# Bucket sums of layer two of a four-layer graph network: blocks of four tiles, added in PSUM by TensorE

## The chip, the cores and the metric

The kernel runs on one core of a Trainium2 chip. The metric is the device time of one execution, in microseconds (us). Before the change it is 17409.68 us, the median of three runs (17409.63 to 17410.06).

## The reference, cut to what matters

Four message-passing layers run on one graph of 12,500 nodes and 400,000 edges sorted by destination. Each layer reads node rows by an index, makes a message per edge, sums the messages per target node, adds the result to `x` and normalises. Layers one, three and four sum by `dst`, which is sorted. Layer two (`_L1_gnn_ref`) is different: it reads by `dst` and sums by `src`, which is random.

```python
edge_index = jnp.stack([src, dst])
# layer two
xj = x[edge_index[1]]
msg = basis[:, 0:1] * (xj @ w2[0])
for k in range(1, k1 * k2):
    msg = msg + basis[:, k:k + 1] * (xj @ w2[k])
out = jax.ops.segment_sum(msg, edge_index[0], num_segments=n_nodes)
```

## The kernel before, in words

Layer two takes two passes. The first (the spread) computes the 32 numbers of each message and scatters the row (33 numbers: the message and the target's number inside its bucket) to a table `pay` in HBM. The nodes are split into 125 buckets of 100; a bucket has some 3,200 edges. Each bucket owns whole tiles of 128 rows there. Rows that no edge fills hold the number -1 and add nothing. These filler rows are written during layer one by SyncE's queue (L2138). The spread is a loop of 125 chunks; its scatters are issued by GpSimd, 25 for each chunk (L1898).

The second pass (the fold) is what the change is about. The tiles are read back in four groups side by side, 825 tiles to a group (`Q1`), in 33 chunks of 25 tiles (`T`) per group. For each tile a one-hot matrix of 128 rows by 100 nodes is made, and TensorE multiplies the 32 message columns with it, which gives 32x100 sums; the four groups are the four column groups of the array, so one tile of each group fills 128 partitions of PSUM (L1728). VectorE then carries a running sum along the tiles: `row[t] = row[t-1] * ms[t] + product[t]`, where `ms` is 0 at the start of a bucket (`vector_sums2`, L783). Each chunk's rows go to a table `fold` in HBM (L1394), from which GpSimd later gathers the last row of each bucket (L1994).

A chunk is worked in five blocks of five tiles (times four groups, 20 one-hots of 100 columns). VectorE makes a block's one-hots in one instruction (L770, 128x2000). ScalarE needs 20 small instructions (L1384) and one large one (L1387). GpSimd needs 20 small ones (L1920). In chunks with an odd number VectorE makes blocks 0, 2, 4, GpSimd block 1 and ScalarE block 3; in even ones VectorE makes 0 and 4, GpSimd 1, ScalarE 2 and 3. There are two row buffers, one one-hot buffer for each block, and four PSUM banks, taken in turn.

The order is written out by hand: each engine has its own program, which waits on counters. `q_y` counts blocks that TensorE has finished, `dv` counts VectorE's instructions (`PER2` of them in a chunk), `q_a` ScalarE's blocks and `po_rows` GpSimd's. TensorE goes through the blocks in order; before a block it waits for its one-hots and for VectorE to have read the bank. A row buffer is loaded again (SyncE's queue, L2092) when TensorE is done with the chunk two before. The buckets' tile numbers are computed on VectorE in `vector_starts` between layers one and two (L596 to L634).

Of the kernel before, what the change touches and what calls it, by code (L numbers as in the profile page):

```python
# [27 lines left out]
Q1 = 825  # L28
NT1 = 4 * Q1
NC1 = Q1 // T  # L30
# [36 lines left out]
def gnn_kernel(nc, x, src, dst, ea2, ea3, ea5, ew, ew1, W0, W1, G2, MU, SG, ROOT, BIAS, w1, b1, w2, b2, out):  # L67

    ctx = ExitStack()
    with ctx:  # L70
# [22 lines left out]
        til_d = dram("til", [NP * 27])  # L93
        fold_d = dram("fold", [P * Q1, NJ])
# [130 lines left out]
        kc = cv(Q1)  # L225
        hb_ = cv(625)
        tot, tls, cum, bst = cv(125), cv(125), cv(125), cv(125)
        tid_i, tid = cv(27, I32), cv(27)
        tilb = cv(27)
        gof, lst = cv(4), cv(2)  # L230
        tli = cv(125, I32)
        big = cv(27 * 25)[0:NP]
# [35 lines left out]
        F1.rows = [cv(4 * 33 * T) for _ in range(2)]  # L268
        F1.rowv = [a.rearrange("p (g t c) -> p g t c", g=4, c=33) for a in F1.rows]
        F1.OH = [cv(20 * NJ) for _ in range(2)]  # L270
        F1.row = [cv(T * NJ) for _ in range(2)]
        F1.ms = [cv(T) for _ in range(2)]
        F1.tail = cv(NJ * 32)[0:3]
        F1.crossT = cv(NP)[0:3]
        F1.OH += [cv(20 * NJ) for _ in range(3)]
        F1.OHv = [a.rearrange("p (g t n) -> p g t n", g=4, t=5) for a in F1.OH]
# [161 lines left out]
        def vector_between(e):  # L438
# [127 lines left out]
        def vector_starts(e):  # L566
# [5 lines left out]
            e.tensor_scalar(tot, tot, 127.0, None, ALU.add).then_inc(dv.up(), 1)  # L572
# [3 lines left out]
            e.tensor_scalar(tli, tli, 7, None, ALU.arith_shift_right).then_inc(dv.up(), 1)  # L576
# [8 lines left out]
            e.tensor_scalar(bst, bst, 128.0, None, ALU.mult).then_inc(dv.up(), 1)  # L585
# [10 lines left out]
            for b in range(0, 125, 25):  # L596
                after(e)
                e.tensor_tensor(
                    big.rearrange("p (t b) -> p t b", t=27), cum[0:NP, b:b + 25].unsqueeze(1).to_broadcast([NP, 27, 25]),
                    tid[0:NP].unsqueeze(2).to_broadcast([NP, 27, 25]), ALU.is_le).then_inc(dv.up(), 1)  # L600
                after(e)
                e.tensor_reduce(bst[0:NP, 0:27], big.rearrange("p (t b) -> p t b", t=27), AX.X, ALU.add).then_inc(dv.up(), 1)
                after(e)
                if b == 0:
                    e.tensor_copy(tilb[0:NP], bst[0:NP, 0:27]).then_inc(dv.up(), 1)
                else:
                    e.tensor_tensor(tilb[0:NP], tilb[0:NP], bst[0:NP, 0:27], ALU.add).then_inc(dv.up(), 1)
# [8 lines left out]
            for r in range(3):  # L616
                e.tensor_scalar(gof[0:NP, r:r + 1], lst[0:NP, 0:1], float(Q1 * (r + 1)), None, ALU.is_ge).then_inc(dv.up(), 1)
                e.tensor_scalar(cross[0:NP, r:r + 1], gof[0:NP, 3:4], float(Q1 * (r + 1) - 1), None, ALU.is_le).then_inc(dv.up(), 1)
# [4 lines left out]
            e.scalar_tensor_tensor(out=lst[0:NP, 0:1], in0=mean[0:NP, 0:1], scalar=float(31 * Q1), in1=lst[0:NP, 0:1], op0=ALU.mult, op1=ALU.add).then_inc(dv.up(), 1)  # L623
# [5 lines left out]
            e.tensor_scalar(var[0:NP, 0:32], io125[0:NP, 0:32], float(Q1), lst[0:NP, 0:1], ALU.mult, ALU.add).then_inc(dv.up(), 1)  # L629
# [3 lines left out]
            e.tensor_tensor(xr[:, 1:Q1], kc[:, 1:Q1], kc[:, 0:Q1 - 1], ALU.is_equal).then_inc(dv.up(), 1)  # L633
# [120 lines left out]
        PER2 = 28  # L754

        def v2_rows(c, b):
            return c * PER2 + (mk["base2"] + {0: 1, 2: 7, 4: 13}[b])

        def v2_sum(c, b):
            return c * PER2 + (mk["base2"] + {0: 12, 1: 18, 2: 23, 3: 28, 4: 34}[b])  # L760

        def numbers2(k, b):

            return F1.rowv[k % 2][:, :, 5 * b:5 * b + 5, 32:33]

        def vector_rows2(e, c, i, k, b):
            if b == 0:
                e.wait_ge(sem(f"ro1_{k % 2}"), nth2(i, k) * 16)
            e.wait_ge(sem("q_y"), c * 5 + (b + 6))
            e.tensor_tensor(F1.OHv[b], numbers2(k, b).to_broadcast([P, 4, 5, NJ]),  # L770
                            iop[:, 0:NJ].unsqueeze(1).unsqueeze(1).to_broadcast([P, 4, 5, NJ]), ALU.is_equal).then_inc(dv.up(), 1)

        def vector_sums2(e, c, i, k, b):
            s2 = k % 2
            e.wait_ge(sem("q_y"), c * 5 + (b + 11))
            if b == 0:
                e.wait_ge(sem("q_m"), c + 1)
                e.wait_ge(sem(f"rowd1_{s2}"), nth2(i, k) * 16)
            for j in range(5):
                t = 5 * b + j  # L780
                so_far = F1.row[s2][:, NJ * t - NJ:NJ * t] if t else F1.row[1 - s2][:, NJ * T - NJ:NJ * T]
                e.wait_ge(dv.h, v2_sum(c, b) - (5 - j) if j else (v2_sum(c, b - 1) if b else v2_sum(c - 1, 4)))
                e.scalar_tensor_tensor(out=F1.row[s2][:, NJ * t:NJ * t + NJ], in0=so_far, scalar=F1.ms[s2][:, t:t + 1],  # L783
                                       in1=ps[(k + b) % 4][:, NJ * j:NJ * j + NJ], op0=ALU.mult, op1=ALU.add).then_inc(dv.up(), 1)

        def vector_chunk2(e, c, i, k):
            i_ = 0 if i is None else i
            vector_rows2(e, c, i_, k, 0)
            if i is None:
                e.wait_ge(dv.h, v2_rows(0, 0))  # L790
                e.sem_inc(dv.up(5), 5)
            else:
                vector_sums2(e, c - 1, i, k - 1, 4)

            vector_rows2(e, c, i_, k, 2 if k % 2 else 4)
            vector_sums2(e, c, i_, k, 0)
            if k % 2:
                vector_rows2(e, c, i_, k, 4)
            else:
                e.wait_ge(dv.h, v2_rows(c, 4) - 1)  # L800
                e.sem_inc(dv.up(), 1)
            for b in range(1, 4):
                vector_sums2(e, c, i_, k, b)

        def vector_fold(e):
# [4 lines left out]
            vector_chunk2(e, 0, None, 0)  # L810
            with e.Fori(0, NC1 // 4) as i:
                for k in range(1, 5):
                    vector_chunk2(e, i * 4 + k, i, k)
            e.wait_ge(dv.h, v2_sum(NC1 - 1, 3))
            e.sem_inc(dv.h, 1)
            vector_sums2(e, NC1 - 1, NC1 // 4 - 1, 4, 4)
            dv.n = v2_sum(NC1 - 1, 4)

# [555 lines left out]
        def scalar_chunk2(e, c, i, k):  # L1374
            s2 = k % 2
            e.wait_ge(dv.h, v2_sum(c - 2, 4))
            e.activation(F1.ms[s2], xr[:, bass.ds(c * T, T)], ACT.Copy).then_inc(sem("q_m"), 1)

            e.wait_ge(sem(f"ro1_{s2}"), nth2(0 if i is None else i, k) * 16)
            for b in (3,) if k % 2 else (2, 3):  # L1380
                e.wait_ge(sem("q_y"), c * 5 + (b + 6))
                for g in range(4):
                    for j in range(5):
                        m = e.activation(F1.OHv[b][:, g, j], io125[:, 0:NJ], ACT.Abs, scale=-1.0, bias=F1.rowv[s2][:, g, 5 * b + j, 32:33])  # L1384
                m.then_inc(sem("q_d"), 1 + k % 2)
                e.wait_ge(sem("q_d"), c * 2 + (b - 1))
                e.activation(F1.OH[b], F1.OH[b], ACT.Relu, scale=-1.0, bias=ones[:, 0:1]).then_inc(sem("q_a"), 1 + k % 2)  # L1387
# [328 lines left out]
        def tensor_chunk2(e, c, k):  # L1716
            s2 = k % 2
            for b in range(5):
                if b in (0, 4) or b == 2 and k % 2:
                    e.wait_ge(dv.h, v2_rows(c, b if k % 2 or b == 0 else 2))  # L1720
                elif b == 1:
                    e.wait_ge(sem("po_rows"), c + 2)
                else:
                    e.wait_ge(sem("q_a"), c * 2 + (b - 1))
                e.wait_ge(dv.h, v2_sum(c, 0) if b == 4 else v2_sum(c - 1, b + 1))
                for j in range(5):
                    for g in range(4):
                        m = e.matmul(ps[(k + b) % 4][32 * g:32 * g + 32, NJ * j:NJ * j + NJ], F1.rowv[s2][:, g, 5 * b + j, 0:32],  # L1728
                                     F1.OHv[b][:, g, j], start=True, stop=True)
                m.then_inc(sem("q_y"), 1)  # L1730

        def tensor_fold(e):
            e.sem_inc(sem("q_y"), 10)
# [177 lines left out]
        def gpsimd_chunk2(e, c, i, k):  # L1911

            s2 = k % 2
            e.wait_ge(sem(f"ro1_{s2}"), nth2(0 if i is None else i, k) * 16)
            held(e)
            e.wait_ge(sem("q_y"), c * 5 + 7)
            held(e)
            for g in range(4):
                for j in range(5):
                    m = e.tensor_scalar(F1.OHv[1][:, g, j], io125[:, 0:NJ], F1.rowv[s2][:, g, 5 + j, 32:33], None, ALU.is_equal)  # L1920
# [344 lines left out]
```

## Time and profile before

| | us |
|---|---|
| median of the runs shown | 17409.68 |
| the profiled execution's own time | 17404.72 |
| its span, first to last instruction | 17402.7 |
| layer one and its ends | up to 4411 |
| the spread | 4411 to 8435 |
| the fold, first load issued to last sum | 8440.2 to 8921.2 |
| layers three and four | from 8975 |

Over the span, VectorE is busy 70%, GpSimd 74%, TensorE 37% and ScalarE 19%. These shares are means over stages that have different limits: in the spread GpSimd issues scatters without a pause, in layer four VectorE and TensorE are busy. Only the fold's own rows speak of the fold.

### The profile page before, as it was taken

The numbers are of one execution on the slowest core, as the hardware profiler recorded it, in microseconds if no ns is written. First come the engines' busy times: TensorE is split into PE (matmuls) and PEld (weight loads), VectorE is DVE, ScalarE is ACT, GpSimd is POOL, SyncE is SP. The second block draws the span as 40 slices with busy tenths as digits, with TensorE's granted clock in tenths as the row PEclk, the third lists the DMA queues.
The fourth block names the chain that finished last, engine by engine and source line by source line (L and its number), as shares of the span: only waits on it lengthen the run. The fifth ranks groups of instructions, "written<-read, shape, count | busy, mean of one in ns | idle before, by whom it ended". The sixth has DMA issues, their size and how long they took to land. (4 is left out here: it accounts for less than half of the span.)

```text
span 17402.7 us, 138752 instructions
## 1 busy us (share of the span) xinstructions
PE 6419.3 (37%) x33487; PEld 5142.6 (30%) x33487; DVE 12117.7 (70%) x15588; ACT 3285.1 (19%) x5336; POOL 12932.6 (74%) x13715
## 2 busy tenths in 40 slices
PE   1000000000444454545330000000006999999995
PEld 0000000000333333333320000000005878878774
DVE  5666666674899999999663232223326999999996
ACT  0000000000222222222541101111102223222321
POOL 6777777777677777777757777777777777777776
PEclk9555555555777777777665555555558999999998
DMA  4333333331111111111332222222222222222221
GB/s 103 97 96 97 97 98 97 98 97 47 28 28 28 28 28 28 28 28 25 130 130 59 59 57 59 58 59 58 59 53 45 55 55 53 56 53 56 53 56 36
DMA packets 744244, 1076.69 MB, mean 62 GB/s; under 512 B 375703, under 2 KB 508493, under 8 KB 731294
## 3 DMA queue, kind: packets, MB, share of 16 engines
q0 software_dynamic: 417376, 477.82, 12.5%
q1 hardware_dynamic: 250851, 398.14, 8.2%
q10 hardware_dynamic: 75736, 197.70, 3.1%
q8 instruction: 88, 1.44, 0.0%
q14 instruction: 193, 1.58, 0.0%
HBM read 684.92 MB, written 389.48 MB: 62 GB/s over the span
## 5 line engine op out<-in xcount | busy, mean ns | idle before, releaser
L1937 POOL DMA_INDIRECT s_arena<-d_t,s_arena x3125 | 3086.5, 988 | 971.3 <-issue 943.6
L1898 POOL DMA_INDIRECT d_pay<-s_arena x3125 | 3026.9, 969 | 997.7 <-issue 931.0
L1977 POOL DMA_INDIRECT s_arena<-d_t,s_arena x3125 | 2960.6, 947 | 1032.6 <-issue 952.0
L1955 POOL DMA_INDIRECT s_arena<-d_t,s_arena x3125 | 2948.5, 944 | 981.7 <-issue 952.1
L1649 PE MATMUL psall<-s_arena 128*128 128x500 bf16 x1875 | 835.4, 500 | 4365.4 <-DVE psall L881 3637.1
L992 DVE TENSOR_TENSOR s_arena<-s_arena,psall 128x2400 f32<-128x2400 f32 x125 | 332.0, 2656 | 2712.1 <-DMA s_arena<-d_t,s_arena 2712.1
L1649 PEld LDWEIGHTS psall<-s_arena 128*128 128x128 bf16 x1875 | 222.5, 119 | 4783.3 <-DVE psall L881 3708.7
L1756 PE MATMUL psall<-s_w2r,s_arena 128*128 128x384 f32 x4250 | 1514.0, 491 | 5.9 <-DVE s_arena L1090 5.2
L1838 PE MATMUL psall<-s_tails,s_mfix 128*128 128x32 f32 x6 | 1.9, 412 | 3972.8 <-DVE s_tails L1198 3972.8
L1756 PEld LDWEIGHTS psall<-s_w2r,s_arena 128*128 128x128 f32 x4250 | 1271.0, 317 | 64.3 <-DVE s_arena L1090 6.1
L1099 DVE TENSOR_REDUCE s_arena<-s_arena 128x64 f32<-128x1024 f32 x875 | 1248.1, 1438 | 0.0
L1838 PEld LDWEIGHTS psall<-s_tails,s_mfix 128*128 128x128 f32 x6 | 1.5, 313 | 3974.0 <-DVE s_tails L1198 3974.0
L1666 PE MATMUL psall<-s_ident,s_arena 128*128 128x128 f32 x3125 | 603.3, 321 | 1406.8 <-DVE s_arena L665 1406.8
L1675 PE MATMUL psall<-s_arena 128*128 128x128 f32 x6250 | 1052.1, 316 | 112.3 <-ACT s_arena L1360 103.5
L901 DVE TENSOR_REDUCE s_arena<-s_arena 128x600 f32<-128x4200 f32 x125 | 1027.2, 8218 | 4.3
L1360 ACT ACTIVATE s_arena<-psall 128x512 f32<-128x512 f32 x875 | 482.7, 552 | 2743.3 <-PE psall L1666 2743.3
L1675 PEld LDWEIGHTS psall<-s_arena 128*128 128x128 f32 x6250 | 906.0, 221 | 309.7 <-DVE s_arena L688 150.6
L564 DVE TENSOR_TENSOR s_arena<-s_arena,psall 128x625 bf16<-128x625 f32 x1250 | 957.7, 801 | 0.0
L890 DVE TENSOR_TENSOR s_arena<-s_arena,psall 128x600 f32<-128x600 f32 x125 | 97.5, 780 | 1172.4 <-DMA s_arena<-d_t,s_arena 1172.4
L1783 PE MATMUL psall<-s_arena,s_ident 128*128 128x256 f32 x4000 | 907.4, 378 | 0.0
L1666 PEld LDWEIGHTS psall<-s_ident,s_arena 128*128 128x128 f32 x3125 | 451.9, 168 | 1430.0 <-issue 1430.0
L1512 ACT ACTIVATE s_arena<-s_arena 128x800 f32<-128x800 f32 x125 | 213.9, 1711 | 3492.9 <-DVE psall L864 3463.7
(304 smaller groups left out, 17923.9 us busy)
## 6 DMA issues: line engine op xcount, KB each, us to landing
s_arena<-d_t,s_arena POOLq DMA_INDIRECT x9375, 2.5
d_scan<-s_arena ACTq DMA_DIRECT2D x313, 400.0 KB, 2.6
s_arena<-d_ew SPq DMA_DIRECT2D x126, 800.0 KB
s_arena<-d_pay SPq DMA_DIRECT2D x33, 1650.0 KB, 6.8
d_inj<-s_agg SPq DMA_DIRECT2D x125, 400.0 KB, 3.9
s_arena<-d_inj SPq DMA_DIRECT2D x125, 400.0 KB, 3.4
d_pay<-s_arena POOLq DMA_INDIRECT x3125, 2.2
d_fold<-s_arena ACTq DMA_DIRECT2D x33, 1250.0 KB, 4.9
```

The source lines that it names most:

```text
L564: return e.tensor_tensor(O[sl], h5[:, :, bass.ds(n, 1)].to_broadcast([P, 5, 125]), iob, ALU.is_equal)
L901: e.tensor_reduce(S[:, :, 8:32], w7.rearrange("p m t c -> p t c m"), AX.X, ALU.add)
L1099: e.tensor_reduce(L3.sums[s2][:, t0:t0 + n].rearrange("p t c -> p (t c)"), prod(g).rearrange("p t (b v) -> p (t b) v", v=16), AX.X, ALU.ad ...
L1649: e.matmul(R5s[:, 0:4], lhsT, rhs[:, 0:4], start=start, stop=True, skip_group_check=True)
L1666: m = e.transpose(ps[6][:, 128 * t:128 * t + 128], S1.xb[:, 128 * (t0 + t):128 * (t0 + t) + 128], ident[:, :])
L1675: m = e.matmul(ps[2 + yb][:, 128 * t:128 * t + 128], S1.xT[yb][:, 128 * t:128 * t + 128], S1.wt, start=True, stop=True)
L1756: m = e.matmul(ps[BANK[g] + t][:, 0:384], hv_[:, :, t0 + t], L3.w2v if g in ONPE else w2r[:, :], start=True, stop=True)
L1783: m = e.matmul(L3.vs, ident[:, :], L3.prodP[:, v], start=v == 0, stop=v == 15, skip_group_check=True)
L1898: e.indirect_dma_start(pay_d, bass.IndirectOffsetOnAxis(ap=S1.adr[s4][:, t:t + 1], axis=0), S1.pay[s4][:, 33 * t:33 * t + 33], None).then_ ...
L1937: e.indirect_dma_start(L3.gb[s][:, t], None, T3_d, bass.IndirectOffsetOnAxis(ap=L3.idx[s][:, t:t + 1], axis=0)).then_inc(sem(f"g3_{s}"), 16)
L1955: e.indirect_dma_start(L0.gb[s][:, t * 128:(t + 1) * 128], None, T0_d, bass.IndirectOffsetOnAxis(ap=L0.idx[s][:, t:t + 1], axis=0)).then_i ...
L1977: e.indirect_dma_start(L2.gb[k][:, t * 96:(t + 1) * 96], None, T2_d, bass.IndirectOffsetOnAxis(ap=L2.idx[k][:, t:t + 1], axis=0)).then_inc ...
```

## The change

A bucket now owns whole blocks of four tiles (512 rows; before it was whole tiles of 128). A chunk has seven blocks (`NBK`) of four tiles (`K4`) per group, 28 tiles; there are still 33 chunks (`NC1`), so the table grows from 3,300 to 3,696 tiles. TensorE adds the four products of a block in one place of PSUM (`start=j == 0`, `stop=j == K4 - 1`), and VectorE's running sum takes one instruction of 128x100 for a block, seven for a chunk. `fold` has seven entries per chunk and group, where it had 25.

The one-hots of a block are now 16 per instruction group (128x1600). In even chunks VectorE makes blocks 0 to 3, ScalarE 4 and 5, GpSimd 6; in odd ones VectorE 0 to 4, ScalarE 5, GpSimd 6. There are four row buffers, and eight one-hot buffers, of which the eighth is block 4's in even chunks. VectorE's sums of blocks 4, 5 and 6 of a chunk stand between its first one-hots of the next one. The fillers in layer one are 30 tiles a chunk, where they were 27. In `vector_starts` five passes of three instructions over 25 buckets become one of two over all 125.

```diff
-Q1 = 825
+K4 = 4
+NBK = 7
+NC1 = 33
+QBK = NBK * NC1
+Q1 = K4 * QBK
...
-        F1.rows = [cv(4 * 33 * T) for _ in range(2)]
+        F1.rows = [cv(4 * 33 * K4 * NBK) for _ in range(4)]
...
-            for b in range(0, 125, 25):
...
+            e.tensor_tensor(
+                big.rearrange("p (t b) -> p t b", t=NTI), cum[0:NP].unsqueeze(1).to_broadcast([NP, NTI, 125]),
+                tid[0:NP].unsqueeze(2).to_broadcast([NP, NTI, 125]), ALU.is_le).then_inc(dv.up(), 1)
...
+        PER2 = 12
+        BY_VECTOR = ((0, 1, 2, 3), (0, 1, 2, 3, 4))
+        BY_SCALAR = ((4, 5), (5,))
...
+        def bank2(k, b):
+
+            return ps[(3 * k + b) % 4]
 
         def vector_rows2(e, c, i, k, b):
             if b == 0:
-                e.wait_ge(sem(f"ro1_{k % 2}"), nth2(i, k) * 16)
-            e.wait_ge(sem("q_y"), c * 5 + (b + 6))
...
+                e.wait_ge(sem(f"ro1_{k % 4}"), nth4(i, k) * 16)
+            e.wait_ge(sem("q_y"), y2(c - 2, 4) if b == 4 else y2(c - 1, b))
+            e.tensor_tensor(F1.OHv[b], number2(k, b).to_broadcast([P, 4, K4, NJ]),
+                            iop[:, 0:NJ].unsqueeze(1).unsqueeze(1).to_broadcast([P, 4, K4, NJ]), ALU.is_equal).then_inc(dv.up(), 1)
+
+        def vector_sum2(e, c, i, k, b):
             s2 = k % 2
-            e.wait_ge(sem("q_y"), c * 5 + (b + 11))
+            e.wait_ge(sem("q_y"), y2(c, b))
...
-            for j in range(5):
...
+            e.wait_ge(dv.h, v2_sum(c, b - 1) if b else v2_sum(c - 1, NBK - 1))
+            e.scalar_tensor_tensor(out=F1.row[s2][:, NJ * b:NJ * b + NJ], in0=so_far, scalar=F1.ms[s2][:, b:b + 1],
+                                   in1=bank2(k, b)[:, 0:NJ], op0=ALU.mult, op1=ALU.add).then_inc(dv.up(), 1)
 
         def vector_chunk2(e, c, i, k):
             i_ = 0 if i is None else i
...
+            for b in range(3):
+                vector_rows2(e, c, i_, k, b)
+                if i is None:
+                    e.wait_ge(dv.h, v2_rows(c, b))
+                    e.sem_inc(dv.up(), 1)
+                else:
+                    vector_sum2(e, c - 1, i, k - 1, 4 + b)
+            vector_rows2(e, c, i_, k, 3)
+            vector_sum2(e, c, i_, k, 0)
+            if 4 in BY_VECTOR[k % 2]:
                 vector_rows2(e, c, i_, k, 4)
...
             for b in range(1, 4):
-                vector_sums2(e, c, i_, k, b)
+                vector_sum2(e, c, i_, k, b)
...
         def scalar_chunk2(e, c, i, k):
...
-            for b in (3,) if k % 2 else (2, 3):
...
+            for b in BY_SCALAR[k % 2]:
+                o = onehot2(k, b)
+                e.wait_ge(sem("q_y"), y2(c - 2, 4) if b == 4 else y2(c - 1, b))
...
         def tensor_chunk2(e, c, k):
...
+                e.wait_ge(dv.h, v2_sum(c, b - 4) if b > 3 else v2_sum(c - 1, b + 3))
+                for j in range(K4):
                     for g in range(4):
...
+                        m = e.matmul(bank2(k, b)[32 * g:32 * g + 32, 0:NJ], F1.rowv[k % 4][:, g, K4 * b + j, 0:32],
+                                     F1.OHv[o][:, g, j], start=j == 0, stop=j == K4 - 1, skip_group_check=True)
...
         def gpsimd_chunk2(e, c, i, k):
...
+            b = NBK - 1
...
+            e.wait_ge(sem("q_y"), y2(c - 1, b))
...
         def sync_chunk2(e, c, k):
...
-            e.wait_ge(sem("q_y"), c * 5 + 5)
...
+            e.wait_ge(sem("q_y"), y2(c - 4, NBK - 1))
```

On VectorE, at the start of a chunk inside the fold's loop, this stood before. `m_ro1_0` is the row load's counter, `m_q_y` TensorE's, `m_dv` VectorE's own.

```order
L768 ISA
L769 ISA [waits m_ro1_0]
L770 TENSOR_TENSOR s_arena<-s_arena,psall 128x2000 [waits m_q_y]
L775 REGISTER_ALU
L782 REGISTER_ALU [waits m_q_y]
L783 SCALAR_TENSOR_TENSOR s_arena<-s_arena,psall 128x100 [waits m_dv]
L782 REGISTER_ALU
L783 SCALAR_TENSOR_TENSOR s_arena<-s_arena,psall 128x100 [waits m_dv]
```

Five sums of the chunk before followed one block of one-hots. At the same place there is now one sum between two blocks:

```order
L781 TENSOR_TENSOR s_arena<-s_arena,psall 128x1600 [waits m_q_y,m_ro1_3]
L786 REGISTER_ALU
L791 REGISTER_ALU [waits m_q_y]
L792 SCALAR_TENSOR_TENSOR s_arena<-s_arena,psall 128x100 [waits m_dv]
L781 TENSOR_TENSOR s_arena<-s_arena,psall 128x1600 [waits m_q_y]
L786 REGISTER_ALU
```

So a single sum stands between large instructions, for blocks 4, 5 and 6 of the chunk before. Each sum has its own wait for TensorE, where one wait served five sums.

On TensorE, the first chunk of the fold read so before (`m_po_rows` is GpSimd's block, `m_q_a` ScalarE's):

```order
L1728 MATMUL psall<-s_arena 32x100 [waits m_bar,m_dv]
L1728 MATMUL psall<-s_arena 32x100 x19
L1728 MATMUL psall<-s_arena 32x100 [waits m_dv,m_po_rows]
L1728 MATMUL psall<-s_arena 32x100 x19
L1728 MATMUL psall<-s_arena 32x100 [waits m_dv,m_q_a]
```

And now, from the chunk's fourth block on:

```order
L1741 MATMUL psall<-s_arena 32x100 [waits m_dv]
L1741 MATMUL psall<-s_arena 32x100 x15
L1741 MATMUL psall<-s_arena 32x100 [waits m_dv,m_q_a]
L1741 MATMUL psall<-s_arena 32x100 x15
L1741 MATMUL psall<-s_arena 32x100 [waits m_dv,m_q_a]
L1741 MATMUL psall<-s_arena 32x100 x15
L1741 MATMUL psall<-s_arena 32x100 [waits m_dv,m_po_rows]
```

GpSimd's block moved from second to last, ScalarE's stand right ahead of it, and VectorE's come first.

## Rows read from the trace of the kernel before

**Rows 1.** The fold: us; PE, PEld, DVE, ACT, POOL busy; clock, DMA share, GB/s
```profile
8440.20:8921.20 481.00, 230.22 (x6600) 209.81 (x6600) 433.04 (x907) 376.07 (x1083) 335.50 (x660) 0.73 0.54 204
```
**Rows 2.** Groups of instructions by line in the fold, 8440 to 8925
```profile
L1920 POOL TENSOR_SCALAR s_arena<-s_io,s_arena 128x100 f32<-128x100 f32 x660 | 335.5, 531 | 144.8 <-PE psall L1728 124.3 <-DMA s_arena<-d_pay 20.5
L1384 ACT ACTIVATE s_arena<-s_io,s_arena 128x100 f32<-128x100 f32 x1000 | 274.0, 364 | 79.0 <-PE psall L1728 72.1 <-DMA s_arena<-d_pay 6.8
L783 DVE SCALAR_TENSOR_TENSOR s_arena<-s_arena,psall 128x100 f32<-128x100 f32 x825 | 262.6, 318 | 38.6 <-PE psall L1728 7.3 <-DVEq L801 4.9 <-DVE s_arena L783 0.5
L1728 PE MATMUL psall<-s_arena 128*32 128x100 f32 x6600 | 230.2, 314 | 354.3 <-DVE s_arena L770 194.9 <-DVEq L791 118.5 <-issue 15.7
L770 DVE TENSOR_TENSOR s_arena<-s_arena,psall 128x2000 f32<-128x2000 f32 x82 | 182.9, 2231 | 9.6 <-DMA s_arena<-d_pay 7.2 <-issue 2.2
L1387 ACT ACTIVATE s_arena<-s_arena,s_ones 128x2000 f32<-128x2000 f32 x50 | 98.2, 1963 | 2.7
L1377 ACT ACTIVATE s_arena<-s_xr 128x25 f32 x32 | 6.9, 216 | 15.6 <-DVE s_arena L783 14.4 <-issue 1.2
```
**Rows 3.** Instructions in order of time, two chunks of the fold, from 8593.6
```profile
8593.61 2.23 DVE L770 TENSOR_TENSOR s_arena<-s_arena,psall 128x2000 f32<-128x2000 f32 x1
...
8595.76 1.73 DVE L783 SCALAR_TENSOR_TENSOR s_arena<-s_arena,psall 128x100 f32<-128x100 f32 x5
...
8595.97 5.19 PE L1728 MATMUL psall<-s_arena 128*32 128x100 f32 x120 [5.03 <-DVE s_arena L770]
8597.40 2.23 DVE L770 TENSOR_TENSOR s_arena<-s_arena,psall 128x2000 f32<-128x2000 f32 x1
...
8599.76 10.17 POOL L1920 TENSOR_SCALAR s_arena<-s_io,s_arena 128x100 f32<-128x100 f32 x20 [3.58 <-PE psall L1728]
8600.41 1.96 ACT L1387 ACTIVATE s_arena<-s_arena,s_ones 128x2000 f32<-128x2000 f32 x1
...
8601.58 5.28 DVE L783 SCALAR_TENSOR_TENSOR s_arena<-s_arena,psall 128x100 f32<-128x100 f32 x15 [0.30 <-DVEq L801]
...
8602.50 1.95 PE L1728 MATMUL psall<-s_arena 128*32 128x100 f32 x80 [1.33 <-ACT s_arena L1387]
8603.64 5.49 ACT L1384 ACTIVATE s_arena<-s_io,s_arena 128x100 f32<-128x100 f32 x20 [1.16 <-PE psall L1728]
...
8616.51 5.27 DVE L783 SCALAR_TENSOR_TENSOR s_arena<-s_arena,psall 128x100 f32<-128x100 f32 x15
...
8616.72 1.08 PE L1728 MATMUL psall<-s_arena 128*32 128x100 f32 x40 [1.04 <-DVE s_arena L770]
...
8621.70 2.23 DVE L770 TENSOR_TENSOR s_arena<-s_arena,psall 128x2000 f32<-128x2000 f32 x1
```
**Rows 4.** Two stretches of 3.5 us of the fold, columns as in rows 1
```profile
8597.10:8600.60 3.50, 3.50 (x92) 3.50 (x88) 3.36 (x6) 3.47 (x14) 0.84 (x2) 0.50 0.08 29
...
8614.70:8618.20 3.50, 2.05 (x84) 1.61 (x76) 3.36 (x6) 3.32 (x13) 3.50 (x8) 1.00 0.03 10
```
**Rows 5.** The page's costliest groups: a smaller VectorE instruction of the same kind
```profile
L890 DVE TENSOR_TENSOR s_arena<-s_arena,psall 128x600 f32<-128x600 f32 x125 | 97.5, 780 | 1172.4 <-DMA s_arena<-d_t,s_arena 1172.4
```
**Rows 6.** Instructions in order of time, the start of the fold
```profile
8435.23 2.14 DVE L807 MEMSET s_arena<- 128x2500 f32 x1 [101.69 <-PEq L159]
8437.84 2.14 DVE L807 MEMSET s_arena<- 128x2500 f32 x1 [0.47 <-issue]
```
**Rows 7.** Time to landing of the fold's row loads (L2092)
```profile
DMA to landing us min/median/max: 6.7/6.8/10.1
```
**Rows 8.** DMA issues by line in the fold and in layer one: KB, us to landing
```profile
d_fold<-s_arena ACTq DMA_DIRECT2D x33, 1250.0 KB, 4.9
...
d_scan<-s_arena ACTq DMA_DIRECT2D x33, 400.0 KB, 2.8
```
**Rows 9.** VectorE's first instruction after `vector_starts`, in order of time
```profile
4165.33 1.03 DVE L1249 TENSOR_TENSOR s_x<-s_x,s_agg 125x768 f32<-125x768 f32 x1 [10.22 <-DMA s_agg<-d_scan,s_endi]
```
**Rows 10.** Who GpSimd waited for, 187 to 4440: total us, times, longest
```profile
POOL s_arena L1955 <- issue: 952.1, 3124, 0.3
```

More of the change, by code:

```diff
@@ L92, in gnn_kernel @@
         pay_d = dram("pay", [P * NT1, 33])
-        til_d = dram("til", [NP * 27])
-        fold_d = dram("fold", [P * Q1, NJ])
+        til_d = dram("til", [NP * NTI])
+        fold_d = dram("fold", [P * QBK, NJ])
         Y_d = dram("y", [P, (TP + T) * 9])
@@ L267, in gnn_kernel @@
         F1 = Spread()
[L268 removed]
+        F1.rows = [cv(4 * 33 * K4 * NBK) for _ in range(4)]
         F1.rowv = [a.rearrange("p (g t c) -> p g t c", g=4, c=33) for a in F1.rows]
[L270 to L272 removed]
+        F1.OH = [cv(4 * K4 * NJ) for _ in range(NBK + 1)]
+        F1.row = [cv(NBK * NJ) for _ in range(2)]
+        F1.ms = [cv(NBK) for _ in range(2)]
         F1.tail = cv(NJ * 32)[0:3]
         F1.crossT = cv(NP)[0:3]
[L275 to L276 removed]
+        F1.OHv = [a.rearrange("p (g t n) -> p g t n", g=4, t=K4) for a in F1.OH]
         assert cv.at <= ARENA
@@ L571, in vector_starts @@
             after(e)
-            e.tensor_scalar(tot, tot, 127.0, None, ALU.add).then_inc(dv.up(), 1)
+            e.tensor_scalar(tot, tot, float(128 * K4 - 1), None, ALU.add).then_inc(dv.up(), 1)
             after(e)
@@ L622, in vector_starts @@
             after(e)
-            e.scalar_tensor_tensor(out=lst[0:NP, 0:1], in0=mean[0:NP, 0:1], scalar=float(31 * Q1), in1=lst[0:NP, 0:1], op0=ALU.mult, op1=ALU.add).then_inc(dv.up(), 1)
+            e.scalar_tensor_tensor(out=lst[0:NP, 0:1], in0=mean[0:NP, 0:1], scalar=float(31 * QBK), in1=lst[0:NP, 0:1], op0=ALU.mult, op1=ALU.add).then_inc(dv.up(), 1)
             after(e)
@@ L813, in vector_fold @@
                     vector_chunk2(e, i * 4 + k, i, k)
[L814 to L817, printed above, removed]
+            for b in range(4, NBK):
+                e.wait_ge(dv.h, v2_sum(NC1 - 1, b - 1))
+                e.sem_inc(dv.h, 1)
+                vector_sum2(e, NC1 - 1, NC1 // 4 - 1, 4, b)
+            dv.n = v2_sum(NC1 - 1, NBK - 1)
         def vector_root(e, b):
@@ L1716, in tensor_chunk2 @@
         def tensor_chunk2(e, c, k):
[L1717 to L1721, printed above, removed]
+            for b in range(NBK):
+                o = onehot2(k, b)
+                if b in BY_VECTOR[k % 2]:
+                    e.wait_ge(dv.h, v2_rows(c, b))
+                elif b in BY_SCALAR[k % 2]:
+                    e.wait_ge(sem("q_a"), c * 2 + (b - 3))
+                else:
                     e.wait_ge(sem("po_rows"), c + 2)
[L1723 to L1726, printed above, removed]
+                e.wait_ge(dv.h, v2_sum(c, b - 4) if b > 3 else v2_sum(c - 1, b + 3))
+                for j in range(K4):
                     for g in range(4):
-                        m = e.matmul(ps[(k + b) % 4][32 * g:32 * g + 32, NJ * j:NJ * j + NJ], F1.rowv[s2][:, g, 5 * b + j, 0:32],
-                                     F1.OHv[b][:, g, j], start=True, stop=True)
+                        m = e.matmul(bank2(k, b)[32 * g:32 * g + 32, 0:NJ], F1.rowv[k % 4][:, g, K4 * b + j, 0:32],
+                                     F1.OHv[o][:, g, j], start=j == 0, stop=j == K4 - 1, skip_group_check=True)
                 m.then_inc(sem("q_y"), 1)
         def tensor_fold(e):
-            e.sem_inc(sem("q_y"), 10)
+            e.sem_inc(sem("q_y"), 3 * NBK)
             barrier(e, "tensor")
```

124 lines of the change are left out of this document (51 added, 73 removed).

## The prediction

> **What bounds the kernel now.** I first read the page's busy slices to find the stage, then the busy time of each engine inside it, then its groups of instructions, and last two chunks in order of time. The fold takes 481.0 us from the first load's issue to the last sum [rows 1]. In it VectorE is busy 433.0 us, which is 90%; ScalarE 78%, GpSimd 70%, TensorE 48%; the DMA engines have a share of 0.54. VectorE's own idle time is small: 38.6 us ahead of the sums and 9.6 ahead of the one-hots, against 354 us for TensorE and 145 for GpSimd, which wait for others [rows 2]. So VectorE sets the pace. Its time is 825 sums of 318 ns (262.6 us) and 82 blocks of one-hots of 2231 ns (182.9 us).
>
> In order of time the reader is to see the spacings, since starts overlap ends a little [rows 3]. A block of one-hots is followed after 2.15 us (8593.61 to 8595.76), 0.08 less than it lasts. Five sums in a row take 1.64 us until the next one-hots start (8595.76 to 8597.40), and fifteen take 5.19 (8616.51 to 8621.70). So one sum that feeds the next costs 0.351 us, and the last before a block of one-hots 0.24 (1.64 less four times 0.351). Two chunks are 28.09 us (8593.61 to 8621.70): five blocks of 2.15, 45 sums of 0.351 and five of 0.24 make 27.7, and one gap of 0.30 behind L801 the rest. This working leaves less than 0.1 us over, so I apply it to the new order.
>
> **VectorE after the change.** It makes nine blocks in two chunks, each 128x1600. No row has that size. Between 600 elements (780 ns) [rows 5] and 2000 (2231 ns) [rows 2] the slope is 1.036 ns, which gives 1816 ns; strict proportion to 2000 gives 1785, and the size left unchanged 2231. I take 1.815, so a spacing of 1.735: nine are 15.6 us. There are 14 sums. Seven stand alone ahead of one-hots (blocks 4, 5, 6 twice, block 0 in odd chunks): 7 x 0.24 = 1.7. The others are a run of four in even chunks and of three in odd ones: 5 x 0.351 + 2 x 0.24 = 2.2. The gap for a bare counter step (it was L801) stays in even chunks: 0.3. That is 19.8 us in two chunks, 9.9 in one, against 14.04.
>
> One new wait comes with it. In an even chunk the sum of block 3 stands right behind the one-hots of block 3, the sums of blocks 0 to 2 and the gap, some 1.3 us later. TensorE needs in that time 0.12 us to start (8595.84 to 8595.97), a block, and 0.1 to report. Forty instructions took 1.08 us with the clock at full (8616.72) [rows 3]; at 2.05 us for 84 [rows 4] eight fewer are 0.2 less, so a block of 32 is 0.9: 1.1 in all and no wait. At the lower level 92 took 3.50 us, 38 ns each [rows 4], so the block is 1.4, and VectorE waits 0.3. Queued behind that sum are the next chunk's one-hots, for which TensorE waits.
>
> The rows show both levels. A burst after 5.03 us of idle [rows 3] ran at 0.50, which is 1.2 GHz, and the one at 8616 at 1.00, which is 2.4 GHz [rows 4]; over the fold the mean is 0.73 [rows 1]. In the new order a block comes every 2 us or less and the long gaps go. The Trainium skill, "TensorE: Matmul & The Clock Gate", section "Loop structure matters more than you think", says that the loop nest decides whether matmuls stay warm, dense ones doing so and those split by waits running cold. By the rule as I read it dense blocks would hold the upper level and a chunk would take 9.9; if the bursts run as the one after idle did, 10.2.
>
> The mean clock lies between, and so do I: 10.05 us a chunk.
>
> **The other engines' loops, which must stay below that.** ScalarE makes three blocks in two chunks. Twenty small ones take 5.49 us [rows 3], 16 then 4.4; the large one 1.6 (from 216 ns at 25 elements and 1963 at 2000) [rows 2]: 6.0 a block, 18.0 for three. With two copies and one wait until TensorE frees the buffer of block 5 (relu's end at 8602.37 to 8603.64, 1.27 us for 40, so 1.1 for 32) [rows 3] it is 19.5 us in two chunks, under 20.1 by only 3%. GpSimd has one buffer: 16 of 20 in 10.17 us is 8.1, plus 0.2 to TensorE, its block and 0.2 back: 9.4 at full clock, 9.9 at the lower level. TensorE runs 7 x 32 = 224 instructions at 24 ns, 5.5 us (8.5 at 38). All are close behind VectorE, which is why my value isn't the 9.9.
>
> **Loads and stores.** A load is 28 tiles in place of 25, 1848 KB in place of 1650; landing goes from 6.8 [rows 7] to 7.6 us, bounded by 6.8 and, at its slowest of 10.1, by 11.3. With four buffers it has some 30 us, so it is hidden. A store shrinks from 1250 to 350 KB. The nearest row for one of that size is 400 KB in 2.8 us, against 4.9 for 1250 [rows 8]. Together the two move 2.2 MB where they moved 2.9, so the DMA engines get less to do in a chunk.
>
> **Start and end.** The first one-hots wait for the first load, 7.6 us. In chunk 0 ScalarE makes two blocks in a row, ready for VectorE at 7.6 + 12.0 + 1.1 = 20.7 us, where VectorE has got to 19.3: 1.4 us. The three sums at the end add 0.5. So the fold takes 33 x 10.05 + 9.5 = 341.2 us, against 481.0: 139.8 less. Ahead of it the barrier waits for two memsets of 2.14 us [rows 6], now of 700 elements: 0.6 each by size, 3.1 less. The last store lands some 2 us sooner [rows 8].
>
> **What costs nothing.** `vector_starts` loses 13 instructions, but VectorE stands idle for 10.22 us behind it, until a gather lands [rows 9]. The longer fillers, 30 tiles for 27, run beside GpSimd's gathers, which wait for nothing but their own issue in 3124 of 3125 cases [rows 10]; if that cover went, 50 KB more at 2.8 us for 400 KB [rows 8] would cost at most 0.35 us each, 44 us for 125. The spread's scatters are as many as before. The gathers from `fold` too.
>
> **Sum.** 139.8 + 3.1 + 2.0 = 144.9 less. The profiled execution took 17404.72 us in all, 17402.7 of it the span, and so gives 17259.8; the median of the runs shown is 5.0 above it. I predict 17265 us.
>
> **Rivals.** (a) ScalarE or GpSimd becomes the bound, each waiting in turn for TensorE, which takes blocks strictly in order. For it: ScalarE's 19.5 of 20.1. Against: their waits now (79.0 and 124.3 us) [rows 2] are time that they can give. At 10.8 us a chunk, with 0.75 x 33 = 25 us more, 17290. (b) The loads set the pace, four of them in flight beside the stores. At 11.3 us a chunk: 17306. Against it stands a share of 0.54 now. (c) Slower: adding in PSUM takes away the overlap of the four column groups, since an instruction that adds to a place must wait for the one before. An instruction would then take four times the 24.4 ns of 84 in 2.05 us [rows 4], 98 ns, and a chunk 224 x 98 ns = 21.9 us: 33 x 11.8 = 391 us over my forecast, 17656. It decides from 63 ns on, where 224 make 14.04 us. Against it: 3300 products are 6600 instructions now [rows 2], so each product is already made of two that add to one place. (d) It doesn't do what it says: the additions saved on VectorE come back as waits, so that a chunk stays at 13 or more. The gain is then under 35 us, 17375 or above. For it speaks only that every engine has one buffer per block; against, that no loop worked out above is over 10.2.
>
> **Chances.** My forecast, 9.7 to 10.4 us a chunk, 0.67; faster than that (shorter one-hots, the clock held) 0.07; (a) 0.15; (b) 0.04; (c) 0.04; (d) 0.03. A difference of 0.2% (35 us) is about what a measurement of this kernel can tell from no change. Faster is then 0.93, within it 0.03, slower 0.04. The range: 9.5 us a chunk gives 17247, and (a) up to 11.0 gives 17296; I take 17246 to 17300, which leaves out (c), (d), most of (b) and the ends of the others.
>
> **What would show it.** Right: VectorE over 92% busy in a fold of about 341 us, one-hots of 1.8 us, 231 sums, nine to two chunks in a steady pattern of one-hots, sum, one-hots; GpSimd and ScalarE waiting shortly for TensorE; the mean clock above 0.73. Wrong: VectorE's sums of blocks 5 or 6 waiting for TensorE, which would be (a); waits for the row loads, (b); a block of 32 on TensorE over 2 us, (c); a change in layers one, three or four.

## The result, and the profile after

The changed kernel takes 17329.07 us, the median of four runs (17328.70 to 17329.95), beside 17409.72 for the kernel before. The ratio is 0.9953 (0.9941 to 0.9965). It is faster by 80.6 us, where I forecast 144.9, and its time lies above my range. The profiled execution spans 17327.5 us, 75.2 less than before.

The fold, with the columns of [rows 1]:

```profile
8438.10:8844.50 406.40, 237.45 (x7392) 205.85 (x7392) 319.18 (x379) 302.64 (x883) 268.62 (x528) 0.78 0.52 185
```

It went from 481.0 to 406.4 us, and the forecast was 341.2. VectorE's 319 us of work fit the forecast (92% of 341 is 314), but they are 79% of the fold, where over 92% was expected. The groups by line answer to [rows 2]:

```profile
L1933 POOL TENSOR_SCALAR s_arena<-s_io,s_arena 128x100 f32<-128x100 f32 x528 | 268.6, 530 | 145.8 <-PE psall L1741 128.7 <-DMA s_arena<-d_pay 17.1
L781 DVE TENSOR_TENSOR s_arena<-s_arena,psall 128x1600 f32<-128x1600 f32 x148 | 268.6, 1815 | 10.1 <-DMA s_arena<-d_pay 7.6 <-PE psall L1741 2.1
L1741 PE MATMUL psall<-s_arena 128*32 128x100 f32 x7392 | 237.5, 289 | 274.1 <-DVEq L801 115.5 <-DVE s_arena L781 65.9 <-issue 65.8
L1396 ACT ACTIVATE s_arena<-s_io,s_arena 128x100 f32<-128x100 f32 x800 | 220.2, 363 | 96.9 <-PE psall L1741 89.7 <-DMA s_arena<-d_pay 7.2
...
L792 DVE SCALAR_TENSOR_TENSOR s_arena<-s_arena,psall 128x100 f32<-128x100 f32 x231 | 72.7, 315 | 77.3 <-PE psall L1741 70.4 <-DVEq L810 5.0
```

VectorE waits for TensorE now, 70.4 us where it was 7.3 [rows 2]. ScalarE and GpSimd wait too, as they did before. TensorE itself has 65.8 us of idle time marked "issue", in which it waits for nothing that the profile shows; it was 15.7 [rows 2]. So no engine's work is the bound. From the table of waits (total us, times, longest), 8440 to 8845:

```profile
DVE s_arena L792 <- PE psall L1741: 70.4, 35, 8.3
PE psall L1741 <- issue: 65.8, 29, 6.1
```

Of the 29, seven last 5.03 to 6.13 us and no other more than 3.03. The fold's loop has eight turns of four chunks, so seven branches back, and each of the seven stands behind one, some 49 us apart. TensorE at the first, in order of time:

```profile
8499.65 1.46 PE L1741 MATMUL psall<-s_arena 128*32 128x100 f32 x26 [0.51 <-issue]
8503.52 0.37 PE L1741 MATMUL psall<-s_arena 128*32 128x100 f32 x1 [2.40 <-DVE s_arena L792]
8510.02 6.62 PE L1741 MATMUL psall<-s_arena 128*32 128x100 f32 x223 [6.13 <-issue]
```

TensorE runs one matmul instruction of the new turn and then stands for 6.13 us, though the block's one-hots are long there. The 2.40 us ahead of it belong to the same pause. The profile puts them down to a sum on VectorE, but the block needs only the sum of block 3 of the chunk before, which was done by 8496.4. So the whole pause runs from the end of the old turn (8501.11) to 8510.02, 8.9 us, where 1.1 us lie between blocks in steady work. The seven are 7.9 to 9.2 us long, 8.5 on average. VectorE behind the first:

```profile
8502.61 1.82 DVE L781 TENSOR_TENSOR s_arena<-s_arena,psall 128x1600 f32<-128x1600 f32 x1
8511.92 0.32 DVE L792 SCALAR_TENSOR_TENSOR s_arena<-s_arena,psall 128x100 f32<-128x100 f32 x1 [7.50 <-PE psall L1741]
```

The sum that waits is that of block 0. VectorE's seven waits behind the seven branches are 6.24 to 8.29 us, 52.0 us together.

The DMA queues show what happens in the pause. These are the packets that start from 8500.5 to 8501.5, from 8501.5 to 8507.5, and from 8507.5 to 8508.5 (in the middle stretch the instruction queue, q8, starts none; q1 carries the row load that was issued at 8501.35):

```profile
q8 instruction: 1, 0.02, 6.0%
```

```profile
q1 hardware_dynamic: 433, 1.60, 81.4%
```

```profile
q8 instruction: 1, 0.02, 6.0%
```

So two pieces of program arrive one after the other, with the load's packets between them. TensorE's single instruction stands behind the first (8503.52), and its steady work behind the second (8510.02).

The kernel before, at the same place of its loop:

```profile
8510.85 6.83 PE L1728 MATMUL psall<-s_arena 128*32 128x100 f32 x200 [6.44 <-DVE s_arena L770]
8524.48 1.54 PE L1728 MATMUL psall<-s_arena 128*32 128x100 f32 x26 [6.80 <-DVE s_arena L770]
8526.69 4.21 PE L1728 MATMUL psall<-s_arena 128*32 128x100 f32 x125 [0.67 <-issue]
```

There 9.0 us pass from 8517.68 to 8526.69, but 6.80 of them are spent waiting for VectorE's one-hots (made from 8522.11 to 8524.35), which come late in any case. The queue of instructions moves the same in both (queue, kind: packets, MB, share). First after, then before:

```profile
q8 instruction: 71, 1.16, 1.2%
```

```profile
q8 instruction: 71, 1.16, 1.1%
```

This gave the theory that I then tested: at each branch back TensorE's program is fetched again by DMA. It was fetched as often before, but beside a wait for VectorE.

Outside the loop the small terms came as forecast. The memsets are one row now:

```profile
8436.53 1.38 DVE L816 MEMSET s_arena<- 128x700 f32 x2 [101.35 <-ACTq L163]
```

From them to the fold's first load pass 3.4 us less (forecast 3.1), and from the last sum to the reads behind it 2.1 less (forecast 2.0). The stages before the fold are 1.3 us longer and those behind it 3.5. That is as much as executions differ: a kernel below with the same stages ahead starts its memsets another 2.2 us later (8438.76).

### The profile page after: what moved, and what is told of

It is laid out like the page before. It is cut to its first block and busy times, and to the rows that moved or that the text cites. A ratio compares the mean times of both kernels' runs of the same rounds, so it can differ in the third digit from the quotient of the medians.

```text
span 17327.5 us, 139047 instructions
## 1 busy us (share of the span) xinstructions
PE 6413.4 (37%) x34279; PEld 5136.3 (30%) x34279; DVE 11996.9 (69%) x15047; ACT 3210.1 (19%) x5136; POOL 12869.2 (74%) x13583
```

## The experiments

"A chunk" is the time between the first and the last store to `fold`, divided by 32, in the one profiled execution of each kernel. Each ratio is to the kernel before on the same chip, with its interval. The chips differ by some 8 us on the kernel before, so ratios or chunks are to be compared, not times. The last two columns are taken between the two stores, and the last is the waits of VectorE's sums alone.

| kernel | time, us | ratio | a chunk, us | TensorE's idle "issue", us | VectorE waits for TensorE, us |
|---|---|---|---|---|---|
| before | 17409.72 | | 14.12 | 15.7 | 1.1 |
| after | 17329.07 | 0.9953 (0.9941 to 0.9965) | 11.92 | 65.8 | 67.1 |
| small loads | 17314.39 | 0.9944 (0.9927 to 0.9960) | 10.82 | 22.3 | 32.5 |
| TensorE unrolled | 17267.73 | 0.9915 (0.9898 to 0.9931) | 9.80 | 1.6 | 1.9 |
| quarter loads | 17307.41 | 0.9938 (0.9921 to 0.9954) | 11.12 | 45.6 | 41.9 |
| loads one block later | 17320.09 | 0.9943 (0.9926 to 0.9961) | 11.49 | 65.8 | 54.0 |
| turn of eight chunks | 17304.27 | 0.9934 (0.9916 to 0.9952) | 11.03 | 52.7 | 37.9 |
| two row buffers | 17357.21 | 0.9966 (0.9953 to 0.9978) | 12.49 | 55.0 | 67.1 |
| two row buffers, seven banks | 17359.81 | 0.9967 (0.9954 to 0.9980) | 12.62 | 62.6 | 66.5 |
| the same, turn of two chunks | 17308.80 | 0.9937 (0.9920 to 0.9955) | 11.04 | 0.6 | 9.2 |
| before, TensorE unrolled | 17410.82 | 0.9999 (0.9990 to 1.0009) | 14.08 | 0 | 0 |
| two row buffers, unrolled | 17317.57 | 0.9946 (0.9930 to 0.9963) | 11.49 | 0.4 | 8.0 |
| old order of blocks, unrolled | 17263.67 | 0.9916 (0.9899 to 0.9933) | 9.78 | 14.1 | 0 |

**Small loads.** Each load in the loop brings 33 numbers of each group (66 KB for 1848), so old rows are summed. The four buffers are filled ahead of the loop, which delays the first one-hots by 17 us (8462.25 for 8445.48).

```diff
-            e.dma_start(F1.rows[s4]..., pay_d...[:, :, bass.ds(c * w, w)])
+            e.dma_start(F1.rows[s4]...[:, :, 0:33], pay_d...[:, :, bass.ds(c * w, 33)])
```

> The changed kernel, but after one full load of the four row buffers each chunk loads only 33 numbers of each group, so nearly no rows move during the fold; one-hots and matmuls are as many, on old rows. Theory F (TensorE runs out of instructions: a turn of its loop is fetched again by DMA, and a fetch stands behind the row loads on the DMA engines): TensorE's idle time with no releaser, 65.8 us in 29 places, falls below 20 us, VectorE's 67 us of waits for TensorE below 20, and a chunk goes from 12.0 to 10.0 to 10.5 us; the fold near 350 us. Rival C (coupling: TensorE takes the blocks strictly in order and ScalarE and GpSimd have one buffer per block, so each waits for the others): rows don't matter to that, the fold stays at 400 us within 5. Rival L (VectorE waits for rows): the fold gets shorter, but no wait for TensorE changes.

A chunk fell to 10.82 us, where 10.0 to 10.5 was expected. The pause stays, and it is shorter:

```profile
8603.00 1.16 PE L1741 MATMUL psall<-s_arena 128*32 128x100 f32 x32 [1.45 <-DVE s_arena L792]
8607.54 0.37 PE L1741 MATMUL psall<-s_arena 128*32 128x100 f32 x1 [3.38 <-DVE s_arena L792]
8610.75 6.95 PE L1741 MATMUL psall<-s_arena 128*32 128x100 f32 x223 [2.83 <-issue]
```

The idle times "issue" over 2 us are seven, all of 2.68 to 3.21 us, again one behind each branch back. The whole pause, with the part ahead of the single instruction, is 6.6 us here (8604.16 to 8610.75), and VectorE's seven waits behind the branches fall from 52.0 to 28.8 us. So traffic of the loads lengthens the pause. It costs some 1.1 us a chunk, and about 1.0 us a chunk over the unrolled kernel is there without it.

**TensorE unrolled.** TensorE's 33 chunks are written out one after the other; the other engines keep their loops.

```diff
-            with e.Fori(0, NC1 // 4) as i:
-                for k in range(1, 5):
-                    tensor_chunk2(e, i * 4 + k, k)
+            for c in range(NC1):
+                tensor_chunk2(e, c, c)
```

> The changed kernel with TensorE's loop over the fold's chunks written out in full (33 chunks in a row, no branch back); all else is the same. Theory F in the form that the branch back is what costs (the fetch ahead is of no use at it): the stall of 5 to 6 us that comes once in a turn of four chunks (8 of them, 44 us) goes, fold 355 to 370 us. Theory F in the form that every piece of the program must be fetched and any of them can come late: as many fetches as before, fold 390 to 405 us. Rival C: no change.

The longest idle time "issue" is 0.7 us now, and a chunk takes 9.80 us. The kernel before took 17415.35 us on this chip, so this one is 147.6 us faster, where the changed kernel is 80.6: the pauses cost 67 us. That is more than the 44 us that I had expected for them. The first load to the last sum takes 339.0 us, where my forecast for the changed kernel was 341.2. VectorE is busy 300.59 of 313.00 us, 96% (columns as in [rows 1]):

```profile
8466.00:8779.00 313.00, 201.15 (x7052) 170.62 (x7040) 300.59 (x362) 284.75 (x831) 256.97 (x506) 0.92 0.60 213
```

In order of time it shows the pattern that I had worked out, here the end of an even chunk:

```profile
8612.96 1.81 DVE L781 TENSOR_TENSOR s_arena<-s_arena,psall 128x1600 f32<-128x1600 f32 x1
8614.69 0.31 DVE L792 SCALAR_TENSOR_TENSOR s_arena<-s_arena,psall 128x100 f32<-128x100 f32 x1
8615.30 1.02 DVE L792 SCALAR_TENSOR_TENSOR s_arena<-s_arena,psall 128x100 f32<-128x100 f32 x3 [0.30 <-DVEq L810]
8616.62 1.82 DVE L781 TENSOR_TENSOR s_arena<-s_arena,psall 128x1600 f32<-128x1600 f32 x1 [0.29 <-PE psall L1741]
```

The last 0.29 us is no wait for TensorE: it stands behind the branch back of VectorE's own loop and comes once in a turn (the kernel before has it as 2.2 us of "issue" ahead of L770 [rows 2]). Where a sum of block 3 does wait, it looks so:

```profile
8636.60 0.32 DVE L792 SCALAR_TENSOR_TENSOR s_arena<-s_arena,psall 128x100 f32<-128x100 f32 x1 [0.57 <-PE psall L1741]
```

Its DMA traffic is the same, at a higher rate (213 GB/s in these 313 us, where the changed kernel has 175 from its first store to its last), and the loads land in 8.5 us for 8.8. So the loads alone are no bound, which disproves rival (b). The instruction queue still moves 58 packets here, but without a branch TensorE hardly waits for them (1.6 us).

**Quarter loads.** Each load is split into four of 462 KB, each with its own wait for TensorE's progress.

```diff
-            e.wait_ge(sem("q_y"), y2(c - 4, NBK - 1))
+            for g in range(4):
+                e.wait_ge(sem("q_y"), y2(c - 4, NBK - 1) + (0, 2, 4, 6)[g])
```

> The changed kernel with each row load issued in four parts of 462 KB, one for each group, spaced over a chunk (each waits for two more blocks of TensorE). The same bytes move. Theory F: a fetch stands behind at most one part (some 2 us in place of 7), so the idle time of TensorE with no releaser falls from 65.8 to 15 to 35 us, fold 355 to 380 us. If what counts is the share of time in which the DMA engines are busy, and not the length of what is queued: unchanged, 400 us. Rival C: unchanged.

```profile
8504.59 0.37 PE L1741 MATMUL psall<-s_arena 128*32 128x100 f32 x1 [4.72 <-DVE s_arena L781]
8507.91 6.35 PE L1741 MATMUL psall<-s_arena 128*32 128x100 f32 x223 [2.95 <-issue]
```

A chunk takes 11.12 us. The second part of the pause is 2.95 us where the changed kernel has 6.13, but the first part is 4.72 where it has 2.40, so the whole falls only from 8.9 to 8.0. VectorE's seven waits fall further, from 52.0 to 34.6 us. The idle time "issue" of 45.6 us is above the 15 to 35 expected. The bytes are the same, so it matters how they lie around the fetch, but less than I had thought.

**Loads one block later.** The load is issued when TensorE has finished the first block of the next chunk.

```diff
-            e.wait_ge(sem("q_y"), y2(c - 4, NBK - 1))
+            e.wait_ge(sem("q_y"), y2(c - 4, NBK - 1) + 1)
```

> The changed kernel with every row load issued when TensorE has done one block more (the first of the next chunk) in place of at the end of block 6, which is the moment of the branch back too. Theory D (of the 5 to 6 us at a branch back, 2.8 are the fetch and the rest is a row load issued at the same moment and standing ahead of it): the big stalls fall to about 2.8 us, as with small loads, and a chunk takes 10.8 to 11.3 us. If the fetch meets the loads by chance and not by this moment: 11.9 as before.

```profile
8602.75 0.37 PE L1741 MATMUL psall<-s_arena 128*32 128x100 f32 x1 [3.23 <-issue]
8606.23 7.46 PE L1741 MATMUL psall<-s_arena 128*32 128x100 f32 x223 [3.11 <-issue]
```

The first part of the pause is put down to "issue" too, here. No piece is over 3.3 us any more, but the sum of the pieces stays (65.8 us in 41), and a chunk takes 11.49 us where at most 11.3 was expected. VectorE's seven waits behind the branches fall from 52.0 to 36.8 us, which is the gain of 0.43 us a chunk. So moving the load off the branch shortens the pause by a third, and what is lost inside a turn stays.

**Turn of eight chunks.** Three branches back where there were seven.

```diff
-            with e.Fori(0, NC1 // 4) as i:
+            with e.Fori(0, NC1 // 8) as i:
```

> The changed kernel with TensorE's loop turning once in eight chunks (4 turns) in place of four (8 turns). Between 12.0 us a chunk with 8 branches back and 9.8 with none, Theory B (each branch back costs its stall, and the rest of the program comes in time) expects half of the loss, 10.9 us a chunk, and 4 stalls of 5 to 6 us. If the length of the program in a turn is what matters (more pieces to fetch), the time stays or rises.

Three idle times of 5.09, 5.25 and 5.14 us stand behind the three branches, and VectorE waits 8.3 to 8.5 us behind each. Four waits fewer at 7.4 us (52.0 in seven) are 30 us, 0.9 a chunk, which makes 11.0; 11.03 was measured. So the loss goes by branches, but for what is lost inside the turns. A longer turn isn't refetched more: the queue moves 67 packets, where it moved 71.

**Two row buffers**, and **seven banks** with them, undo parts of the change on the way to a shorter turn.

```diff
-        F1.rows = [cv(4 * 33 * K4 * NBK) for _ in range(4)]
+        F1.rows = [cv(4 * 33 * K4 * NBK) for _ in range(2)]
```

> The changed kernel with two row buffers, as before the change; a load is issued when TensorE is done with the chunk two before. In the steady state a load still starts behind block 6 of a chunk, one per chunk, so Theory F expects the same stalls, fold 400 us within 8; a rival in which four loads in flight are what delays the fetches expects a fold of 350 to 375 us; if two buffers make VectorE wait for rows (a load lands in 8.8 us of a chunk's 12), the fold is over 410 us with waits for d_pay.

```diff
-            return ps[(3 * k + b) % 4]
+            return ps[b]
```

> Control for the next one: the changed kernel with two row buffers and with seven PSUM banks, one for each block, so that the program repeats every two chunks; TensorE's loop still turns once in four. Two buffers alone gave 12.5 us a chunk with 8 big stalls; with more banks TensorE runs further ahead, 12.0 to 12.5 expected.

Two row buffers cost 0.57 us a chunk: VectorE waits 17.6 us for loads and ScalarE 54.2, and the pauses stay. Three more banks bring nothing (12.62 for 12.49, just above the 12.0 to 12.5 expected): while the pauses stand, the place to put a sum isn't short.

**Turn of two chunks**, on top of two buffers and seven banks.

```diff
-            with e.Fori(0, NC1 // 4) as i:
-                for k in range(1, 5):
+            with e.Fori(0, NC1 // 2) as i:
+                for k in range(1, 3):
```

> As the control with seven banks and two buffers, but TensorE's loop turns once in two chunks (16 turns, some 900 instructions in each in place of some 1,850). If the engine keeps a turn of this length and doesn't fetch it again, the instruction queue moves about 10 packets in the fold in place of 71, no stall without a releaser is left, and a chunk takes 10.5 to 11 us (two buffers make VectorE and ScalarE wait for rows). If every branch back costs a fetch whatever the length, there are 16 stalls, and a chunk takes 13.5 us or more.

This changes TensorE's loop alone against the kernel above, and makes 15 branches back where there were seven. The instruction queue, 8438 to 8925:

```profile
q8 instruction: 6, 0.10, 0.1%
```

It was 78 packets. So 72 of them were TensorE's program fetched again, nine for each of the eight turns, and a turn of two chunks is kept where one of four isn't. TensorE's idle time "issue" goes from 62.6 to 0.6 us, and a chunk from 12.62 to 11.04. What is left is a wait for two buffers' loads (27.5 us on VectorE, 43.0 on ScalarE). That settles the theory: 15 branches leave 0.6 us of idle time "issue" in all, so a branch costs only where the program isn't there any more.

**The kernel before, TensorE unrolled.** The same edit as above, on the kernel before.

> The kernel before, with TensorE's loop over the fold's chunks written out in full. It fetched as much (71 packets) and branched back as often as the changed one. If the stalls were hidden there because VectorE set a pace of 14.0 us and TensorE had time to catch up: a chunk goes from 14.12 to 14.0 us, the whole kernel to within 10 us of before. If they cost then what they cost now: a gain of 50 us or more.

The ratio is 0.9999 (0.9990 to 1.0009): the idle time "issue" of 15.7 us goes, and nothing that can be measured is gained (0.04 us a chunk). The fetch was hidden there. In the changed kernel the same edit is worth 67 us.

**Two row buffers, TensorE unrolled.**

> The changed kernel with TensorE's loop written out and two row buffers in place of four: what the two further buffers are worth once the stalls are gone. With four it was 9.80 us a chunk; the short loop with two and seven banks had 11.04 with waits for rows. Expected 10.8 to 11.2 and waits for d_pay of 40 us or more on ScalarE. If the buffers are worth nothing by themselves: 9.8.

A chunk takes 11.49 us, above the 10.8 to 11.2 expected and 1.69 more than with four buffers, since VectorE waits for loads:

```profile
DVE s_arena L781 <- DMA s_arena<-d_pay: 44.4, 22, 3.9
```

So the four buffers are worth 1.69 us a chunk when nothing else holds it up, and 0.57 with the pauses; that the pauses gave the loads time is my reading. Why this kernel is slower than the turn of two chunks with seven banks (11.49 for 11.04) stays open: they differ in the banks and in the form of the loop, and no run parts the two.

**The old order of blocks, TensorE unrolled.** GpSimd makes block 1, ScalarE 5 and 6, VectorE the rest.

```diff
-        BY_VECTOR = ((0, 1, 2, 3), (0, 1, 2, 3, 4))
-        BY_SCALAR = ((4, 5), (5,))
+        BY_VECTOR = ((0, 2, 3, 4), (0, 2, 3, 4, 5))
+        BY_SCALAR = ((5, 6), (6,))
```

> The changed kernel with TensorE's loop written out and the blocks of a chunk in an order as before the change: VectorE 0, GpSimd 1, VectorE 2 to 4 (5 in odd chunks), ScalarE last (5 and 6, or 6). Each engine makes as many blocks. If the order matters little where VectorE sets the pace: 9.8 to 10.0 us a chunk. If TensorE, in strict order, then waits for GpSimd's block with VectorE's behind it: 10.5 us or more, with VectorE's sums waiting for TensorE.

9.78 us a chunk for 9.80. The new order of the engines is worth nothing measurable. What was gained comes then from fewer sums and from the buffers; the buffers' part was measured above, and that of the sums is argued from VectorE's time, since no run takes them back alone. This and the unrolled kernel beat both kernels of the case.

## Why the prediction was wrong, by its own steps

**The failed step** is the paragraph on the other engines' loops. It gave TensorE 5.5 us a chunk, 224 instructions at 24 ns, and no term for getting them. [Rows 2] had 15.7 us of TensorE's idle time put down to "issue"; I quoted the row and priced only its waits for VectorE. The missing term is 2.12 us a chunk (11.92 less 9.80, the latter measured with the same work and no branches): 68 us in 32 chunks. The fold's miss is 65.2 us (406.4 less 341.2), so this is all of it. Of the 68, 52 are VectorE's seven waits behind the branches; the rest is shorter waits inside the turns, which go with the unrolling too and of which no run shows more. About 1.0 of the 2.12 is the fetch by itself and 1.1 the row loads that delay it, by the run with small loads; that run also has less traffic at all other times, so the split is an estimate, the sum isn't.

With that term taken away the forecast holds: the unrolled kernel is 147.6 us faster than the kernel before on its chip, and I had forecast 144.9.

The Trainium skill, "Runtime: NRT & Kernel Launch", section "🔬 Instruction fetch mechanics", says that an engine's instructions come by DMA in blocks of 16 KiB and that a taken branch to a place outside the window held in the engine waits for a fetch. The trace agrees on both: 71 packets with 1.16 MB are 16.3 KB each, and the pause stands behind the branch. What the section calls mostly hidden is the step from one block to the next in straight code, and the unrolled kernel agrees (58 packets, 1.6 us of idle time). For the branch it gives no price; here it was 7.9 to 9.2 us, hidden before and not after.

**VectorE's own time** was right. One-hots of 1600 take 1815 ns (forecast 1.815), what follows them starts after 1.73 us (1.735), a lone sum takes 0.23 (0.24), and the gap behind the bare step is 0.30. The unrolled kernel's 9.80 a chunk stands beside 9.9 for the clock at full; the mean clock there is 0.92. The new wait for TensorE ahead of block 3's sum is absent in most even chunks; it came in three of them, 0.54 to 0.57 us each (8636.60).

**The clock.** Its mean is 0.92 in the unrolled loop, where blocks come every 2 us, and 0.78 in the changed kernel's fold, where pauses break them up. By the Trainium skill's "Loop structure matters more than you think", in "TensorE: Matmul & The Clock Gate", dense matmuls stay warm; the trace agrees. As the split between 9.9 and 10.2 it moved my forecast by little, and VectorE's 96% shows that it wasn't the limit. The 10.2 itself was wrong: one wait of 0.3 in two chunks adds 0.15 to a chunk, which gives 10.05, and the middle would have been 9.98. That is 2 us in the fold.

**ScalarE and GpSimd.** Their loops were to be "close behind". ScalarE's 16 small ones took 4.41 us (forecast 4.4), the large one 1.63 (1.6), GpSimd's 16 took 8.13 (8.1). In the unrolled kernel ScalarE is busy 91% and GpSimd 82%, with no wait of VectorE behind them.

**The rivals.** (a) had much of the symptom, sums of VectorE waiting for TensorE with both others waiting as well, though the long waits are at the sum of block 0 and not of 5 or 6. It did not have the cause: with the engines' order and work unchanged, unrolling removes them. At 10.8 us a chunk it was also too cheap. (b) fell as a bound by itself; the loads take part by standing ahead of the fetch. (c) fell: a block of 32 instructions takes 0.89 us in the unrolled kernel, 28 ns each, as the forecast's 0.9. (d) said that waits would take the place of the saved sums, and 67 us of them did, for a reason that it didn't name; it had a chunk of 13 and more, and the chunk is 11.92. (By my own sum a chunk of 13 is 17362 us, not 17375.)

**What cost nothing** did so: `vector_starts` is hidden (VectorE now stands idle for 19.43 us ahead of the gather that ends the wait, at 4166.07), and the stages before the fold moved by 1.3 us. The loads land in 8.8 us where I had 7.6; four buffers hide it. The stores land in 5.9 us where I had 2.8, and nothing waits for them inside the fold.

## What to carry to other kernels

Look at how long a written-out loop turn is on each engine, and at idle time with no releaser, or with one that was done long before, just behind the branch back: here a turn of 448 matmuls was fetched anew each time (9 blocks), and one of 224 never. Such a fetch costs nothing while the engine would wait anyway, so before an edit that makes the bound engine faster, price it (here 8.5 us on TensorE at each turn, 7.4 on VectorE) against the wait that covers it now. A large load that is issued at the moment of the branch makes it worse; a shorter turn, or none, took it away. Between 224 and 448 matmuls nothing was tried. Nor was it tried how the pause depends on where a turn begins inside a piece of the program, though TensorE ran one matmul instruction before it stood again here, and 26 in the kernel before.

## What the runs showed of the hardware that I had not expected

A turn of two chunks (224 matmuls, which are 448 matrix records and as many weight loads) is kept by TensorE: 6 instruction packets in the whole fold. A turn of four is not: 71. Straight code for all 33 chunks, 58 packets, shows no idle time "issue" over 0.7 us. The pause comes in two parts with one matmul instruction between them: 2.40 and 6.13 us when a row load of 1848 KB was issued at the branch (8501.35 us, 0.2 us behind the turn's end), 3.38 and 2.83 us with loads of 66 KB. The profile put the first part down to VectorE in most cases, so an idle time with a named releaser can be a fetch too. The instruction queue's share of the DMA engines is 1.2% meanwhile, so its price can't be read from its bytes.
